# High and low matmuls of a split-precision recurrent block: alternating, or in runs of four, eight and sixteen

## The chip, the cores and the metric

The kernel runs on one core of a Trainium2 chip. The metric is the device time of one execution in microseconds (us). Profiles are of one execution. The engines are TensorE (PE, with its weight loads shown apart as PEld), VectorE (DVE), ScalarE (ACT), GpSimd (POOL) and SyncE (SP), which issues transfers.

## The reference, cut to what matters

The input x has 8 x 1024 rows of 256 float32 values. For each row:

```
xn = layernorm(x)
s  = rfs(xn) @ rfs(win)                       # random features, 256 x 256
h  = silu(xn @ w1.T * w1_s) * (xn @ w2.T * w2_s)   # gated layer, 256 -> 1024
h  = gelu(h @ h1.T * h1_s)                    # square layer, 1024 -> 1024
h  = gelu(h @ h2.T * h2_s)                    # square layer, 1024 -> 1024
y  = h @ w3.T * w3_s                          # last layer, 1024 -> 256
out = x + s * silu(y)
```

The weights w1, w2, h1, h2 and w3 hold only -1, 0 and 1. The result is wanted in float32 quality.

## The kernel before, in words

**Splitting.** Each activation is scaled and split into a high part (type float32r, made by ScalarE) and a low part (float16, made by VectorE as the value less its high part). Each product of the layers is then two matmuls into the same bank of PSUM: one with the high part and the weights as float32r, one with the low part and the weights read as bfloat16. The code calls them g = 0 and g = 1. The order of the two is what the change is about.

**Tiles.** A tile is 1024 rows, two halves of 512 (h0 and h1); eight tiles (t = 0 to 7) follow each other. In a tile TensorE goes through these stages, in one queue in this order:
- gated layer by seven products (`gate_seven`, line 850, all tiles but the first): the first half of the hidden columns, for both halves of rows, with Strassen's scheme. Products (p, n), p = 0 to 3 and n = 0 to 6, stand in eight rounds (`ROUNDS`): round i holds (0, i), (1, i), (2, i-1), (3, i-1), as far as n runs from 0 to 6. Each is one high and one low matmul of 512 columns. ScalarE copies the banks of n = 0, 2 and 4 out (lines 1077, 1079, 1081), VectorE adds others to them (1525, 1528, 1532). Product n = 5 waits for the copy of n = 4 of its p (`g3_kept`).
- gated layer by steps (`gate_step`, line 775): a step makes one block of 128 hidden columns for 512 rows: for each of w1 and w2 two high matmuls and then two low ones, into a pair of banks. ScalarE takes the silu (1066), VectorE multiplies (1514). Eight steps a tile, sixteen in the first.
- `dots` (860, the first tile only), `mix` (876) for s.
- two square layers (`product`, line 915), L = 0 and 1. Each is seven block products w = 0 to 6 (Strassen's scheme again, `FAST`): a 512 x 512 block of weights by 1024 rows folded to 512 columns. A product has four output blocks m (bank 4(w % 2) + m) by four contraction blocks k, by high and low: 32 matmuls of 512 columns. The weights of block k come in a piece of 256 KB in a ring of eight buffers, so a product's pieces are loaded while the one before it runs; a piece is given back (`piece_used`, `prod`) at its last use, and SyncE (GpSimd for some pieces of the first tile) then loads the piece of two products later (`feed`, line 453).
- last layer (`down`, line 972): four parts (b11, b22, b12, b21) of four blocks b of 128 rows by four k by high and low: matmuls of 256 columns whose stationary side is the activation. Between them, in all tiles but the last, seven float32 matmuls for the next tile's s (`seven`, lines 928 to 950).

**What a product's banks go through.** Products w = 0, 1 and 3 begin banks; w = 2 adds onto the banks of w = 0, w = 5 onto those of w = 3, and w = 4 and 6 onto those of w = 2. ScalarE copies the banks of w = 0, 2 and 4 to SBUF (`p1_kept`, `u2_kept`, `u3_kept`; lines 1171 to 1175); VectorE adds the bank of w = 1 (line 1590), that of w = 3 to the copy of w = 4 (line 1593, `c_sum["b22"]`), and that of w = 5 (line 1597); ScalarE applies gelu (lines 1163 and 1177). TensorE waits per m before it writes a bank: for w = 5 on `c_sum["b22"]` of m, which needs the copy of w = 4 of m, the product just before. For w = 0 of L = 1 it waits on the gelu of b21, which reads the banks of w = 6 of L = 0, again the product just before. For the others a whole product lies between.

**Order on ScalarE and VectorE.** Both go in program order, m by m: for m = 0 and 1 first the high (1119) or low (1557) split of half of the next product's operand, then the work on bank m of the current product, then the gelu of the block before. In L = 1 at m = 3 of w = 3 and 4 the split of b11 for the last layer stands ahead of the bank's work (`high_last`, line 1134; `low_last`, line 1563). On odd m of tiles 1 to 7, while there are any, ScalarE has a step of `look` (lines 1194 to 1200), which looks over the weights. VectorE has the layernorm of the next tile in L = 0 (`next_rows`; line 1419 normalises, at m = 2 and 3 of w = 4 two blocks each) in tiles 0 to 6.

The heart of `product`:

```
for m in range(Q):
    ... wait for bank m
    for k in range(Q):
        on.wait_ge(*fed[n])
        for g in range(2):
            ... matmul of (m, k), high for g = 0, low for g = 1
```

Of the kernel before, what the change touches and what calls it, by code (L numbers as in the profile page):

```python
# [5 lines left out]
P = 128  # L6
D = 256
# [93 lines left out]
def build(nc, x, win, proj, cols_in, w3s_in, wT, out):  # L101
# [4 lines left out]
    with ExitStack() as ctx:  # L106
# [647 lines left out]
        def _(e):  # L754
# [34 lines left out]
            def gate_step(t, n):  # L789
                h, m = step_of(t, n)  # L790
                pair = (PAIRS if t else PAIRS0)[n]
                on.wait_ge(rows_hi, n_rows_hi(h))
                if h == 0:
                    on.wait_ge(rows_hi0, 1)
                if t == 0:
                    for i in range(2):
                        on.wait_ge(d_w12[i][w12_part(m)], 16)
                gate_banks_free(t, n, 0)
                if h == 0 and m == 0:
                    gate_product(pair[0], w1, h, m, 0, True, False)  # L800
                    gate_product(pair[1], w2, h, m, 0, True, False)
                    on.wait_ge(rows_lo, n_rows_lo(h))
                    gate_product(pair[0], w1, h, m, 1, False, True).then_inc(gate_mm, 1)
                    gate_product(pair[1], w2, h, m, 1, False, True).then_inc(gate_mm, 1)
                else:
                    on.wait_ge(rows_lo, n_rows_lo(h))
                    gate_product(pair[0], w1, h, m, 0, True, False)
                    gate_product(pair[0], w1, h, m, 1, False, True).then_inc(gate_mm, 1)
                    gate_banks_free(t, n, 1)
                    gate_product(pair[1], w2, h, m, 0, True, False)  # L810
                    gate_product(pair[1], w2, h, m, 1, False, True).then_inc(gate_mm, 1)
# [10 lines left out]
            def gate_seven(t):  # L822
# [6 lines left out]
                for p, n in sum(ROUNDS, []):  # L829
# [3 lines left out]
                    if n < 2:  # L833
# [14 lines left out]
                    for g, (x_, T_) in enumerate(((xT_hi, T_hi), (xT_lo, T_lo))):  # L848
                        moving = (x_[0][:, 0, :], x_[0][:, 1, :], T_[:, 1, :], T_[:, 0, :], T_[:, 2, :], T_[:, 3, :], x_[1][:, 1, :])[n]
                        mm = e.matmul(ps[:, bank, :], short(weights) if g else weights, moving, start=n in (0, 1, 3) and g == 0, stop=n in (1, 5, 6) and g == 1,  # L850
                                      skip_group_check=True)
                    mm.then_inc(strassen_mm, 1)
# [27 lines left out]

            def product(t, L, w):
                slot = (t + L + w) % 2
                first, last = FAST[w][1] in ("b11", "b21", "t1"), w in (1, 5, 6)
                on.wait_ge(lo, n_split(t, L, w, 1))
                for m in range(Q):
                    if w == 0 and L == 0:
                        if t == 0:
                            on.wait_ge(*((turned_f, 4) if m < 2 else ((silu, gated)[m - 2], 2 * KH - 1)))
                        elif m % 2 == 0:
                            on.wait_ge(silu, n_step(t, 6 + m // 2))  # L890
                        else:
                            on.wait_ge(gated, n_gate(*step_of(t, 6 + m // 2)))
                    elif w == 0:
                        on.wait_ge(gelu["b21"], n_block(t, 0, m))
                    elif w == 1 and L == 0:
                        on.wait_ge(mixed, 4 * t + m + 1)
                    elif w == 1:
                        on.wait_ge(c_sum["b12"], n_block(t, 0, m))
                    elif w == 2:
                        on.wait_ge(p1_kept, n_block(t, L, m))  # L900
                    elif w == 3:
                        on.wait_ge(c_sum["b11"], n_block(t, L, m))
                    elif w == 4:
                        on.wait_ge(u2_kept, n_block(t, L, m))
                    elif w == 5:
                        on.wait_ge(c_sum["b22"], n_block(t, L, m))
                    else:
                        on.wait_ge(u3_kept, n_block(t, L, m))
                    for k in range(Q):
                        n = n_used(t, L, w, 0) // (Q - 1) * Q + k  # L910
                        on.wait_ge(*fed[n])
                        for g in range(2):
                            weights = ring[n % RING][:, m * P:(m + 1) * P]
                            weights, moving = (weights, slots_hi[slot][:, k, :]) if g == 0 else (short(weights), slots_lo[slot][:, k, :])
                            mm = e.matmul(ps[:, 4 * (w % 2) + m, :], weights, moving,  # L915
                                          start=first and k == 0 and g == 0, stop=last and k == Q - 1 and g == 1, skip_group_check=True)
# [36 lines left out]
            def down(t):  # L953
                begun = set()
                dot = 0
                for n, (name, j, kq) in enumerate(order_of(t)):
                    slot = last_slot(t, name)
                    on.wait_ge(last_lo, n_last(t, LAST[name], 1))
                    on.wait_ge(d_w3, 16)
                    last = j in begun  # L960
                    for b in range(NB):
                        bank, col = y_place(2 * t + j, b)
                        if not last and col == 0:
# [4 lines left out]
                        for k in range(Q):  # L968
                            for g in range(2):
                                tokens, moving = slice(b * P, (b + 1) * P), w3[:, Q * kq + k, :]  # L970
# [955 lines left out]
```

## Time and profile before

| | us |
|---|---|
| median of 3 runs | 1310.86 |
| lowest and highest | 1308.68, 1311.36 |
| the profiled execution | 1308.7 |
| its span, first to last instruction | 1306.9 |
| mean granted TensorE clock | 0.999 of full |
| TensorE busy in the span | 1296.6 (99%), 6010 matmuls |
| VectorE busy | 975.5 (75%) |
| ScalarE busy | 914.7 (70%) |
| GpSimd busy | 291.7 (22%) |

Busy times of matmuls overlap, since the end of one is recorded some 0.18 us after its last column went in, when the next already streams. The spacing of matmuls is therefore read from the chain that ended last: there each stretch of one engine and line stands with its start, its length and how many instructions it holds. In the tables, "idle before <-" names what ended the engine's idle time just before an instruction.

### The profile page before, as it was taken

How to read it: one execution, taken by the hardware profiler on the slowest of the kernel's cores; microseconds unless marked ns; L12 is line 12 of the kernel's file. 1: busy time of each engine (PE TensorE's matmuls, PEld its weight loads, DVE VectorE, ACT ScalarE, POOL GpSimd, SP SyncE). 2: the span in 40 equal slices, each digit the busy share in tenths (PEclk: the TensorE clock that was granted, in tenths of full speed). 3: DMA queues.
4: the chain of work that ended last, by engine and by line, in shares of the span. 5: the costliest groups of instructions: out<-in, count | busy, mean ns of one | idle time of the engine just before them, and what ended most of it. 6: DMA issues, size and time to landing. Idle time of an engine off the chain costs nothing.

```text
span 1306.9 us, 16520 instructions
## 1 busy us (share of the span) xinstructions
PE 1296.6 (99%) x6010; PEld 665.5 (51%) x6010; DVE 975.5 (75%) x1343; ACT 914.7 (70%) x1384; POOL 291.7 (22%) x323
## 2 busy tenths in 40 slices
PE   9999999999999999999999999999999999999998
PEld 5544455444554455544555445554455544554445
DVE  7778777777777787777876777767778677785675
ACT  5465666778667786677776777757777677686664
POOL 7875013110131101311023110322004120050000
PEclk9999999999999999999999999999999999999999
DMA  9689832575125741367414573146631566214441
GB/s 344 245 311 291 289 135 97 158 214 180 68 97 179 219 159 65 116 183 214 141 65 137 166 237 114 65 142 190 208 113 65 169 177 213 94 49 161 149 156 36
DMA packets 97350, 209.47 MB, mean 160 GB/s; under 512 B 13424, under 2 KB 16624, under 8 KB 96240
## 3 DMA queue, kind: packets, MB, share of 16 engines
q1 hardware_dynamic: 80032, 156.98, 36.2%
q0 software_dynamic: 17232, 51.39, 13.2%
q8 instruction: 49, 0.80, 0.2%
q14 instruction: 37, 0.30, 0.1%
HBM read 175.78 MB, written 38.83 MB: 164 GB/s over the span
## 4 chain that ended last, share of the span: by engine, by line
PE 98%; DMA 1%; DVE 1%; ACT 0%; issue 0%
PE ps L915 63%; PE ps L775 10%; PE ps L972 9%; PE ps L850 7%; PE ps L876 4%; DMA ring<-hs 1%; PE ps L860 1%; PE ps L950 0%; PE ps L939 0%; PE ps L928 0%; PE ps L943 0%; PE ps L936 0%; PE ps L947 0%; PE ps L931 0%; DMA xin<-in_x 0%; DVE split_lo L1563 0%
## 5 line engine op out<-in xcount | busy, mean ns | idle before, releaser
L915 PE MATMUL ps<-split_hi,ring 128*128 128x512 f32 x1792 | 833.2, 582 | 1.0 <-DMA ring<-hs 1.0
L915 PE MATMUL ps<-split_lo,ring 128*128 128x512 f16 x1792 | 700.1, 391 | 0.0
L1557 DVE SCALAR_TENSOR_TENSOR split_lo<-quad,split_hi 128x1024 f16<-128x1024 f32 x224 | 277.1, 1243 | 193.0 <-ACT split_hi L1119 193.0
L915 PEld LDWEIGHTS ps<-split_lo,ring 128*128 128x128 bf16 x1792 | 173.2, 97 | 460.1 <-issue 460.0
L915 PEld LDWEIGHTS ps<-split_hi,ring 128*128 128x128 f32 x1792 | 361.2, 202 | 1.6 <-DMA ring<-hs 1.3
L1119 ACT ACTIVATE split_hi<-quad 128x1024 fp32r<-128x1024 f32 x224 | 232.0, 1050 | 39.3 <-PE ps L915 39.3
L1163 ACT ACTIVATE quad<-quad,cols_s 128x512 f32<-128x512 f32 x192 | 135.4, 716 | 41.9 <-DVE quad L1590 22.6
L1582 DVE TENSOR_TENSOR quad<-quad 128x1024 f32<-128x1024 f32 x128 | 154.4, 1241 | 3.8 <-POOL res L616 3.7
L610 POOL TENSOR_TENSOR quad<-quad,s 128x256 f32<-128x256 f32 x56 | 61.8, 1133 | 426.8 <-ACT quad L1155 426.8
L775 PE MATMUL ps<-xT_hi,w 128*128 128x512 f32 x288 | 116.5, 486 | 0.8 <-ACT xT_hi L1222 0.8
L775 PE MATMUL ps<-xT_lo,w 128*128 128x512 f16 x288 | 87.5, 386 | 0.0
L972 PE MATMUL ps<-w,split_hi 128*128 128x256 f32 x272 | 79.7, 398 | 0.1
L596 POOL DMA_DIRECT2D z_h<-xin x56 | 55.6, 1000 | 105.0 <-DVE xin L1419 105.0
L1171 ACT ACTIVATE quad<-ps 128x512 f32<-128x512 f32 x64 | 38.2, 596 | 55.0 <-PE ps L915 54.8
L628 POOL DMA_DIRECT2D seen<-in_h x32 | 17.6, 550 | 246.0 <-ACT signs L1200 246.0
L972 PE MATMUL ps<-w,F_hi 128*128 128x256 f32 x240 | 70.0, 396 | 0.0
L972 PE MATMUL ps<-w,split_lo 128*128 128x256 bf16 x272 | 68.4, 288 | 0.0
L775 PEld LDWEIGHTS ps<-xT_hi,w 128*128 128x128 f32 x288 | 54.5, 190 | 20.3 <-ACT xT_hi L1222 1.0
L1066 ACT ACTIVATE rows<-ps,cols_s 128x512 f32<-128x512 f32 x72 | 49.7, 691 | 17.7 <-PE ps L775 11.5
L972 PE MATMUL ps<-w,F_lo 128*128 128x256 bf16 x240 | 60.4, 288 | 0.0
L972 PEld LDWEIGHTS ps<-w,split_hi 128*128 128x128 f32 x272 | 54.2, 199 | 6.9 <-issue 5.3
L1175 ACT ACTIVATE quad<-ps 128x512 f32<-128x512 f32 x64 | 38.2, 596 | 26.7 <-PE ps L915 25.1
(204 smaller groups left out, 1802.2 us busy)
## 6 DMA issues: line engine op xcount, KB each, us to landing
ring<-hs SPq DMA_DIRECT2D x428, 256.0 KB, 3.5
xin<-in_x SPq DMA_DIRECT2D x16, 512.0 KB, 4.3
s_h<-s SPq DMA_DIRECT2D x16, 512.0 KB, 4.1
seen<-in_h POOLq DMA_DIRECT2D x32, 256.0 KB, 3.9
res<-in_x SPq DMA_DIRECT2D x15, 512.0 KB, 5.4
out<-res SPq DMA_DIRECT2D x15, 512.0 KB, 2.9
z_h<-xin POOLq DMA_DIRECT2D x56, 128.0 KB, 4.2
xT_hi<-z_h POOLq DMA_DIRECT2D x14, 512.0 KB, 5.6
```

Source lines behind the costliest of these rows:

```text
L596: e.dma_start(z_h[j][:, :, :, c, :].rearrange("a i n j -> i n a j"), xin[j][32 * c:32 * c + 32, :, :].rearrange("i b (k a j) -> i (b k) a ...
L610: e.tensor_tensor(y_of(h)[:, b, :], y_of(h)[:, b, :], s[h % 2][:, b, :], ALU.mult).then_inc(pool_y, 1)
L775: mm = e.matmul(ps[:, bank, :], weights, moving, start=first and k == 0, stop=last and k == KD - 1, skip_group_check=h == 0 and m == 0)
L850: mm = e.matmul(ps[:, bank, :], short(weights) if g else weights, moving, start=n in (0, 1, 3) and g == 0, stop=n in (1, 5, 6) and g == 1, ...
L876: mm = e.matmul(ps[:, banks[b // 2], (b % 2) * D:(b % 2 + 1) * D], quad[at[t][0]["v"]][:, KD * j + r, b * P:(b + 1) * P], WS[:, r, :], sta ...
L915: mm = e.matmul(ps[:, 4 * (w % 2) + m, :], weights, moving, start=first and k == 0 and g == 0, stop=last and k == Q - 1 and g == 1, skip_g ...
L972: mm = e.matmul(ps[:, bank, col:col + D], part[:, k, tokens], moving, start=not last and col == 0 and k == 0 and g == 0, stop=last and k = ...
L1066: e.activation(stage[n % 2][:, :], ps[:, (PAIRS if t else PAIRS0)[n][0], :], ACT.Silu, scale=scale_col(0, m)).then_inc(silu, 1)
L1119: e.activation(both(slots_hi[i], g), both(quad[at[t][L][name]], g), ACT.Identity, scale=POWER[L]).then_inc(hi, 1)
L1163: e.activation(q[:, m, :], q[:, m, :], ACT.Gelu, scale=col).then_inc(gelu[name], 1)
L1557: e.scalar_tensor_tensor(out=both(slots_lo[i], g), in0=both(quad[at[t][L][FAST[w][1]]], g), scalar=POWER[L], in1=both(slots_hi[i], g).bitc ...
L1582: e.tensor_tensor(dst, a, b, ALU.subtract).then_inc(block_sum, 1)
```

## The change

The loops over g (high, low) go outward.
- Square layers: all 16 high matmuls of a product, then all 16 low ones. The waits for the banks stand in the high run, in the order of m; the wait for the low split stands before the low run, and the product begins after the high split alone. A bank is handed on (`prod`) after its last low matmul, and pieces are given back in the low run of m = 3.
- Last layer: for each two blocks b, eight high matmuls, then eight low ones.
- Gated layer by steps: the four high matmuls of w1 and w2, then the four low ones; the second bank is waited for after two matmuls rather than four. The very first step was so already, but for the wait's place.
- Gated layer by seven: a round's high matmuls (four, two in the first and the last round), then its low ones, with the waits in the high run.

What is computed, and how many instructions there are, stays.

```diff
@@ gate_step
-                if h == 0 and m == 0:
...
-                else:
-                    on.wait_ge(rows_lo, n_rows_lo(h))
-                    gate_product(pair[0], w1, h, m, 0, True, False)
-                    gate_product(pair[0], w1, h, m, 1, False, True).then_inc(gate_mm, 1)
-                    gate_banks_free(t, n, 1)
-                    gate_product(pair[1], w2, h, m, 0, True, False)
-                    gate_product(pair[1], w2, h, m, 1, False, True).then_inc(gate_mm, 1)
+                gate_product(pair[0], w1, h, m, 0, True, False)
+                gate_banks_free(t, n, 1)
+                gate_product(pair[1], w2, h, m, 0, True, False)
+                on.wait_ge(rows_lo, n_rows_lo(h))
+                gate_product(pair[0], w1, h, m, 1, False, True).then_inc(gate_mm, 1)
+                gate_product(pair[1], w2, h, m, 1, False, True).then_inc(gate_mm, 1)
@@ gate_seven
-                for p, n in sum(ROUNDS, []):
+                for p, n, g in [(p, n, g) for turn in ROUNDS for g in range(2) for p, n in turn]:
...
-                    if n < 2:
+                    if g:
+                        pass
+                    elif n < 2:
                         first_free(t, bank)
...
-                    for g, (x_, T_) in enumerate(((xT_hi, T_hi), (xT_lo, T_lo))):
...
-                    mm.then_inc(strassen_mm, 1)
+                    x_, T_ = (xT_lo, T_lo) if g else (xT_hi, T_hi)
...
+                    if g:
+                        mm.then_inc(strassen_mm, 1)
@@ product (the waits on banks, unchanged, are now bank_free)
-                on.wait_ge(lo, n_split(t, L, w, 1))
-                for m in range(Q):
...
+                on.wait_ge(hi, n_split(t, L, w, 1))
+                for m, g in [(m, g) for g in range(2) for m in range(Q)]:
+                    if g == 0:
+                        bank_free(t, L, w, m)
                     else:
-                        on.wait_ge(u3_kept, n_block(t, L, m))
+                        on.wait_ge(lo, n_split(t, L, w, 1))
                     for k in range(Q):
                         n = n_used(t, L, w, 0) // (Q - 1) * Q + k
                         on.wait_ge(*fed[n])
-                        for g in range(2):
...
-                        if k == Q - 1:
+                        if g and k == Q - 1:
                             mm.then_inc(prod, 1)
-                        elif m == Q - 1:
+                        elif g and m == Q - 1:
                             mm.then_inc(piece_used, 1)
@@ down
-                    on.wait_ge(last_lo, n_last(t, LAST[name], 1))
+                    on.wait_ge(last_hi, n_last(t, LAST[name], 1))
                     on.wait_ge(d_w3, 16)
                     last = j in begun
-                    for b in range(NB):
+                    for b, g in [(b, g) for two in (0, 2) for g in range(2) for b in (two, two + 1)]:
                         bank, col = y_place(2 * t + j, b)
-                        if not last and col == 0:
+                        if g:
+                            on.wait_ge(last_lo, n_last(t, LAST[name], 1))
+                        elif not last and col == 0:
...
-                            for g in range(2):
...
-                        mm.then_inc(down_mm, 1)
-                        if b % 2 and t < END and dot < 7:
-                            seven(t, dot)
-                            dot += 1
+                        if g:
+                            mm.then_inc(down_mm, 1)
+                            if b % 2 and t < END and dot < 7:
+                                seven(t, dot)
+                                dot += 1
```

## Rows read from the trace of the kernel before

**Rows 1.** The page, parts 1 and 4: busy us, share and count; the chain by engine.
```profile
PE 1296.6 (99%) x6010; PEld 665.5 (51%) x6010; DVE 975.5 (75%) x1343; ACT 914.7 (70%) x1384; POOL 291.7 (22%) x323
...
PE 98%; DMA 1%; DVE 1%; ACT 0%; issue 0%
```

**Rows 2.** TensorE's waits (us in total, times, longest), and the ring's transfers.
```profile
PE ps L915 <- DMA ring<-hs: 1.0, 1, 1.0
...
DMA to landing us min/median/max: 2.6/3.5/9.8
```

**Rows 3.** The chain in order of time, tiles 3 and 4: start us, us, what.
```profile
538.84 104.03 PE ps L915 x448
642.87 1.97 PE ps L972 x16
...
664.67 13.01 PE ps L850 x56
677.68 14.60 PE ps L775 x64
```

**Rows 4.** Timeline of TensorE: the first step's low run, and one low matmul.
```profile
10.39 1.04 PE L775 MATMUL ps<-xT_lo,w 128*128 128x512 f16 x4
...
600.21 0.39 PE L915 MATMUL ps<-split_lo,ring 128*128 128x512 f16 x1
```

**Rows 5.** Timeline of ScalarE, tile 3, L = 1, around the end of w = 4.
```profile
626.18 0.60 ACT L1175 ACTIVATE quad<-ps 128x512 f32<-128x512 f32 x1
626.68 0.71 ACT L1163 ACTIVATE quad<-quad,cols_s 128x512 f32<-128x512 f32 x1
627.29 1.05 ACT L1134 ACTIVATE F_hi<-quad 128x1024 fp32r<-128x1024 f32 x1
628.24 0.59 ACT L1175 ACTIVATE quad<-ps 128x512 f32<-128x512 f32 x1
628.71 0.72 ACT L1163 ACTIVATE quad<-quad,cols_s 128x512 f32<-128x512 f32 x1
629.33 0.62 ACT L1200 ACTIVATE signs<-seen 128x512 bf16<-128x512 f32 x1
629.85 0.20 ACT L1200 ACTIVATION_READ_ACCUMULATOR signs<-seen 128x1 f32 x1
```

**Rows 6.** Timeline of VectorE in the same stretch.
```profile
623.75 0.68 DVE L1593 TENSOR_TENSOR quad<-ps,quad 128x512 f32<-128x512 f32 x1
624.35 1.22 DVE L1557 SCALAR_TENSOR_TENSOR split_lo<-quad,split_hi 128x1024 f16<-128x1024 f32 x1
...
628.37 1.23 DVE L1563 SCALAR_TENSOR_TENSOR F_lo<-quad,F_hi 128x1024 f16<-128x1024 f32 x1 [0.86 <-ACT F_hi L1134]
629.51 0.69 DVE L1593 TENSOR_TENSOR quad<-ps,quad 128x512 f32<-128x512 f32 x1
```

**Rows 7.** The chain in order of time, tile 0, the transfer of a piece.
```profile
86.28 9.76 DMA ring<-hs
```

**Rows 8.** Timeline of TensorE: the matmul that this transfer released.
```profile
96.09 0.50 PE L915 MATMUL ps<-split_hi,ring 128*128 128x512 f32 x1 [1.01 <-DMA ring<-hs]
```

**Rows 9.** Timeline of VectorE, tile 3, L = 0: two normalisations and what follows.
```profile
582.89 0.73 DVE L1419 TENSOR_SCALAR xin<-xin,mv,sm 128x256 f32<-128x256 f32 x2
583.54 0.69 DVE L1597 TENSOR_TENSOR quad<-ps,quad 128x512 f32<-128x512 f32 x1
```

**Rows 10.** Timeline of ScalarE in the gated layer by seven products, tile 4.
```profile
671.72 1.09 ACT L1081 ACTIVATE quad<-ps 128x512 f32<-128x512 f32 x2
```

**Rows 11.** The chain in order of time, the last tile's last layer.
```profile
1285.98 2.37 DVE split_lo L1563 x2
1288.35 0.04 issue
```

**Rows 12.** Weight loads of the last layer by form; transposes in the chain.
```profile
L972 PEld LDWEIGHTS ps<-w,F_hi 128*128 128x128 f32 x240 | 47.9, 200 | 5.1 <-issue 5.1
...
15.09 0.87 PE ps L768 x8
```

More of the change, by code:

```diff
@@ L879, in mix, with bank_free @@
                         mm.then_inc(mix_mm, 1)
+            def bank_free(t, L, w, m):
+                if w == 0 and L == 0:
+                    if t == 0:
+                        on.wait_ge(*((turned_f, 4) if m < 2 else ((silu, gated)[m - 2], 2 * KH - 1)))
+                    elif m % 2 == 0:
+                        on.wait_ge(silu, n_step(t, 6 + m // 2))
+                    else:
+                        on.wait_ge(gated, n_gate(*step_of(t, 6 + m // 2)))
+                elif w == 0:
+                    on.wait_ge(gelu["b21"], n_block(t, 0, m))
+                elif w == 1 and L == 0:
+                    on.wait_ge(mixed, 4 * t + m + 1)
+                elif w == 1:
+                    on.wait_ge(c_sum["b12"], n_block(t, 0, m))
+                elif w == 2:
+                    on.wait_ge(p1_kept, n_block(t, L, m))
+                elif w == 3:
+                    on.wait_ge(c_sum["b11"], n_block(t, L, m))
+                elif w == 4:
+                    on.wait_ge(u2_kept, n_block(t, L, m))
+                elif w == 5:
+                    on.wait_ge(c_sum["b22"], n_block(t, L, m))
+                else:
+                    on.wait_ge(u3_kept, n_block(t, L, m))
             def product(t, L, w):
@@ L911, in product @@
                         on.wait_ge(*fed[n])
-                        for g in range(2):
[L913 to L916, printed above, removed]
-                        if k == Q - 1:
+                        weights = ring[n % RING][:, m * P:(m + 1) * P]
+                        weights, moving = (weights, slots_hi[slot][:, k, :]) if g == 0 else (short(weights), slots_lo[slot][:, k, :])
+                        mm = e.matmul(ps[:, 4 * (w % 2) + m, :], weights, moving,
+                                      start=first and k == 0 and g == 0, stop=last and k == Q - 1 and g == 1, skip_group_check=True)
+                        if g and k == Q - 1:
                             mm.then_inc(prod, 1)
-                        elif m == Q - 1:
+                        elif g and m == Q - 1:
                             mm.then_inc(piece_used, 1)
@@ L968, in down @@
                         for k in range(Q):
[L969 to L978 removed]
+                            tokens, moving = slice(b * P, (b + 1) * P), w3[:, Q * kq + k, :]
+                            part, moving = (slots_hi[slot], moving) if g == 0 else (slots_lo[slot], short(moving))
+                            mm = e.matmul(ps[:, bank, col:col + D], part[:, k, tokens], moving,
+                                          start=not last and col == 0 and k == 0 and g == 0, stop=last and k == Q - 1 and g == 1,
+                                          skip_group_check=True)
+                        if g:
[3 more added lines that the diff above has]
+                                dot += 1
                     begun.add(j)
```

36 lines of the change are left out of this document (3 added, 33 removed).

## The prediction

> **What bounds the kernel now.** The page's first part comes first: TensorE is busy for 99% of the span, VectorE for 75%, ScalarE for 70% [rows 1]. The chain that ended last says the same: 98% of it is TensorE [rows 1]. In the table of waits TensorE waits once for a piece of weights (1.0 us) and hardly elsewhere [rows 2]. So the time is the number of matmuls times their spacing, and the change touches both sides: the spacing (which kind follows which), and the distance between the matmul that ends a bank and the one that needs it again.
>
> The spacing stands in the chain in order of time [rows 3]. Square layers: 448 matmuls, 224 pairs of high and low in turn, take 104.03 us, 0.4644 us a pair. Second half of the gated layer: 64 matmuls in runs of two (two high, two low), 14.60 us, 0.4563 a pair or 0.9125 for four. Both orders hold one high-to-low and one low-to-high step per run; the run of two adds one high-after-high and one low-after-low, together 0.9125 - 0.4644 = 0.448. The kernel's first step has a run of four lows [rows 4]: 1.04 us, less 0.39 for one alone, over three steps: 0.217. So high after high is 0.231, and a change of kind costs about 0.008 each way.
>
> **What the longer runs give.** All on TensorE, which sets the end.
> - Square layers: a product of 32 matmuls goes from 7.430 to 0.464 + 15 x 0.448 = 7.186; 0.244 x 112 products = 27.4 us.
> - Gated layer by steps: 1.825 to 0.464 + 3 x 0.448 = 1.809; 0.016 x 71 steps = 1.1 us (one step had this order already).
> - Gated layer by seven products: 28 pairs took 13.01 us [rows 3]. The rounds hold 2, 4 (six times) and 2 pairs: 2 x 0.9125 + 6 x 1.809 = 12.68; 0.33 x 7 tiles = 2.3 us.
> - Last layer: 256 columns, 1.97 us for 8 pairs, 0.2466 a pair [rows 3]; 64 runs of eight. No row has two highs in a row at 256 columns. If a step saves the same 16 ns: 7 x 64 x 0.0163 = 7.3 us; if it halves with the columns, 3.7. I take 5.5, between them. The bound the other way is a rival below.
> Sum: 36.3 us off. The instructions are the same in number, on every engine and queue; TensorE's waits are moved, none is new in kind.
>
> **What it puts in their place.** A bank now ends late. In a product, bank m ended after 8(m+1) of 32 matmuls; now in the low run, after 20, 24, 28 and 32. It is still asked for early, at the product's high run, now at matmul 4m instead of 8m. Where the next product takes the same values on, the distance falls from 24 matmuls (5.6 us) to 12 (2.7 us). That is product w=5 of a layer, which waits for c_sum b22 of the same m: ScalarE copies bank m of w=4 (L1175), VectorE adds (L1593). I walk both queues in program order by the starts in the rows (one start to the next): copy 0.49, gelu 0.61, high split 0.95, look 0.52, VectorE's sum 0.60, low split 1.14 [rows 5, 6]. With E = 0 the end of w=4, banks end at -2.59, -1.73, -0.86, 0. From a release to the end of the matmul that waited is 0.54 us [rows 7, 8] (landing 86.28 + 9.76 = 96.04, record from 96.09, 0.50 long), against 0.23 in the stream, so bank m must be free by 0.93m - 0.30.
> - Layer 2 (L=1). ScalarE: copy 0 at -2.56, high split of w=5, copy 1 at -1.11, gelu, look, copy 2 at 0.52, gelu, then the split of b11 for the last layer (L1134, [rows 5]) 1.62 to 2.67, copy 3 at 2.57. VectorE: low split until 0.17, sum 1 done 0.86 (wanted 0.63), sum 2 done 1.84, then L1563 from 2.70, which waits for that split, and sum 3 done 4.53, wanted 2.48. TensorE stands 0.2 at m=1 and 1.8 at m=3: 2.05 us. Six tiles 12.3, the last (no looks) 1.9, the first (small sums of the projection before sum 2) 2.3: 16.5 us.
> - Layer 1 (L=0). No such split, but two normalisations (L1419, 0.73 for both, 0.64 without the overlap with what follows) before each of sums 2 and 3 [rows 9]: done 0.86, 2.11, 3.36 against 0.63, 1.56, 2.48; 0.88 us in tiles 1 to 6, 0.3 in the last: 5.6. In tile 0 it hides behind the piece (below).
> - Layer 1's w=6 to layer 2's w=0 use one bank as well (gelu b21, then reuse); that walk ends at 0.28, 1.49, 2.07 against 0.63, 1.56, 2.48: nothing, by under 0.1 us. The split of w=1 and of w=3 lands within 0.1 us of its need; nothing too. What covers these is ScalarE being free; if it slips 0.3 us, each costs that.
> - Gated layer by seven: n=5 follows n=4 of its p by one round and needs the copy L1081. The distance falls from 6 matmuls (1.4 us) to 3 (0.7), the copy alone takes 0.60, two together 1.09, so they follow each other by 0.48 [rows 10], and both p of a round wait: 0.30 + 0.26 in round 5, 0.25 + 0.26 in round 6, 1.07 us; x 7 = 7.5. The other waits there are 11 matmuls (2.5 us) and hold.
> - Tile 0: the piece that lands at 96.04 after 9.8 us is the fourth of w=5 [rows 7]. It was wanted after six matmuls, now after three, and TensorE comes 1.5 us sooner. It stands until 96.04 again, has 29 matmuls to go, not 26, and the gains up to there (1.8 us) are lost; the fourth piece of layer 2's w=0 repeats it. 2.6 us in all (between 1, if the transfer starts and lands sooner with the product that frees its buffer, and 4).
> - Later tiles: ring releases bunch at the product's end, up to 0.7 us later, wanted up to 0.7 sooner; median landing is 3.5 us [rows 2] of a product's 7.2. Nothing. Waiting for the high split alone at a product's start, and for the low one 3.7 us later, removes a need that cost nothing.
> - The last tile waited for low splits at 1288.35 in the last layer [rows 11]; with gelus of b21 bunched it waits 0.3 us more.
> Sum: 16.5 + 5.6 + 7.5 + 2.6 + 0.3 = 32.5 us on.
>
> **The number.** 36.3 off and 32.5 on: 3.8 us less. The profiled execution took 1308.7 (span 1306.9 and 1.8 around it); 1304.9 in its place. The median shown, 1310.86, lies 2.2 above it, so 1307.
>
> **Rivals.**
> 1. The waits hardly appear (12%): the queues catch up, or a wait is overlapped as the walk does not see. Against it: the walk uses starts of one execution and strict program order. 36.3 less some 10 gives 1285, all of it 1275.
> 2. Slower: in the last layer a high load does not fit behind 256 columns (10%). The records of high loads last 200 ns [rows 12]; if the next matmul must wait for load and hand-over, high after high is 0.23, as at 512 columns, a pair 0.23 + 0.109 = 0.34 instead of 0.2466, and 448 such steps cost 41 us: 1354. It decides from a pair of about 0.243, where the forecast gain is gone. Against it: eight transposes of 128 float32 columns, each with a load of its own, take 0.87 us, 0.109 each [rows 12], and in the alternating order a load of each kind fits in 0.2466 with a matmul that alone takes half of that. The Trainium skill (TensorE: Matmul & The Clock Gate, LDWEIGHTS) gives columns over 1.2 GHz, an estimate of 107 ns for 128 columns; by it this rival falls, and the records' 200 ns include more than the load.
> 3. Slower: the bunched banks push ScalarE and VectorE behind by more than I walked (18%), at the three places with under 0.1 us to spare. 0.3 us at each, some 40 times, is 12 us: 1319.
> 4. Order does not set the spacing (3%): both orders would have one pair time and only the waits stay, less the 1.8 of gains that tile 0 then has not to lose: 1342. The two pair times in rows 3 speak against it. The Trainium skill (same page, Back-to-back issue gap) has columns over 2.4 GHz plus 2.5 ns whatever the order, 216 ns at 512; the low run's 0.217 agrees, the high run's 0.231 and the alternating 0.232 do not.
> That the order is not what the code says is excluded: one queue, one order.
>
> **How the numbers follow.** The forecast case, waits and gains within a quarter of the walk, has 57% and reaches from 16 us faster to 4 slower, 1295 to 1315. 0.2% is 2.6 us, about what can be told from no change. Three fifths of that case lie beyond it on the fast side, a quarter inside. That gives 0.34 faster, 0.14 same and 0.09 slower; rival 1 adds 0.12 to faster, rivals 2 and 4 0.13 to slower, and rival 3 0.14 to slower and 0.04 to same: 0.46, 0.18, 0.36. The range takes in rival 3 and the near part of rival 1: 1291 to 1320.
>
> **What would show it.** In the chain, a product of w=0 to 4 near 7.19 us; among the waits a new row of L1593 releasing the square layers' matmuls, some 20 us, longest near 1.8, in pairs of places 52 us apart; a second of L1081 releasing the seven products, some 7 us; runs of 16 in the last layer near 1.88 us. A last-layer run at 2.6 would be rival 2; idle time under 10 us on TensorE rival 1; square products at 7.43 without waits rival 4; many short waits for the high split L1119 rival 3.

## The result, and the profile after

| us | before | after |
|---|---|---|
| median of 8 runs each, in turn on one chip | 1309.36 | 1314.78 |
| lowest and highest | 1308.47, 1311.36 | 1312.04, 1317.24 |
| the profiled execution | 1308.7 | 1312.04 |
| its span | 1306.9 | 1310.2 |

The ratio is 1.0038, 95% interval 1.0026 to 1.005: slower by 5.4 us, and beyond the 0.2% of the prediction. Forecast were 1307 and "faster" as the likeliest. The result lies inside the range, on its other side.

TensorE's share fell from 99% to 97%, and the chain that ended last, 98% TensorE before [rows 1], now passes through ScalarE, VectorE and the DMA queues. From the page of after, parts 1 and 4:

```profile
PE 1277.2 (97%) x6010; PEld 813.4 (62%) x6010; DVE 973.5 (74%) x1343; ACT 906.0 (69%) x1384; POOL 294.6 (22%) x323
...
PE 81%; ACT 6%; DVE 6%; DMA 4%; issue 1%; SPq 1%; ACTq 0%; DVEq 0%
```

TensorE's waits of after (us in total, times, longest). Where [rows 2] has a single row for the ring, these matter:

```profile
PE ps L917 <- DVE quad L1597: 13.4, 11, 1.5
PE ps L917 <- DMA ring<-hs: 5.6, 6, 1.8
PE ps L917 <- ACT split_hi L1123: 1.8, 6, 0.8
...
PE ps L975 <- ACT quad L1181: 1.0, 1, 1.0
```

The table undercounts: a matmul held up by less than its own recorded length (0.4 to 0.5 us) shows no idle time. So a wait is read here from how long a product takes, from the end of the last matmul before it to its own last. The windows below are cut at those ends: tile 3, L = 1, products w = 1 to 6 of after. Behind each stretch stands its length (the product's time), then TensorE's busy time; then weight loads, VectorE, ScalarE, GpSimd, the granted clock, the DMA share and GB/s.

```profile
600.76:607.90 7.14, 7.14 (x33) 4.47 (x33) 6.30 (x8) 4.93 (x9) 1.52 (x3) 1.00 0.99 288
607.90:617.00 9.10, 7.70 (x33) 4.43 (x33) 3.79 (x5) 5.47 (x10) 0.00 (x0) 1.00 0.55 174
617.00:624.14 7.14, 7.14 (x32) 4.15 (x31) 5.08 (x6) 4.99 (x9) 0.54 (x1) 1.00 0.71 226
624.14:631.73 7.59, 7.39 (x33) 4.75 (x34) 7.59 (x8) 5.73 (x11) 0.00 (x0) 1.00 0.49 168
631.73:640.96 9.23, 7.73 (x34) 4.26 (x33) 7.16 (x10) 8.20 (x15) 0.00 (x0) 1.00 0.36 115
640.96:648.07 7.11, 7.11 (x35) 4.50 (x34) 3.76 (x6) 5.36 (x9) 0.00 (x0) 1.00 0.45 148
```

An undisturbed product takes 7.14 us, where it took 7.43 (104.03 / 14, [rows 3]). Three here take longer: w = 2 (9.10), w = 4 (7.59) and w = 5 (9.23); in L = 0 only w = 5 does, 8.06. Only w = 5 was forecast. Added up over the 112 products of the profiled execution (each less 7.14):

| place | waits, us | forecast |
|---|---|---|
| w = 5 of L = 1, eight tiles | 16.8 | 16.5 |
| w = 5 of L = 0, tiles 1 to 7 | 5.9 | 5.6 |
| w = 5 of L = 0, tile 0 (not a piece, see below) | 2.2 | 2.6 more than before's 1.3, with the next row |
| w = 0 of L = 1, tile 0 (not a piece) | 1.1 | in the row above |
| w = 2 of L = 1, tiles 1 to 6 | 7.6 | nothing |
| w = 4 of L = 1, tiles 1 to 6 | 2.6 | nothing |
| single pieces (w = 4 of L = 1 in tile 0, w = 3 in tile 6) | 0.4 | nothing |

112 products save 0.29 each, 32.5 us. The table comes to 36.6 (small differences of other products are 0.1), and before itself had 1.3 of waits in tile 0. So the square layers came out 2.7 us longer.

In tile 0 the waits for a piece that were forecast did not come: the fourth piece of w = 5 of L = 0 landed at 93.3, 6.6 us after its issue, for 96.04 before. TensorE waited at the same places for VectorE and ScalarE. TensorE's waits of after, in the window 90 to 112:

```profile
PE ps L917 <- DVE quad L1597: 1.4, 2, 0.7
PE ps L917 <- ACT split_hi L1123: 0.8, 1, 0.8
```

Ahead of each of the sums of banks 2 and 3, VectorE has four statistics of the next tile's rows there (L1429 and L1430, 1.3 us for four). Ahead of w = 0 of L = 1, four normalisations (L1423, 1.4 us) stand before a sum (L1601), and the gelu and the high split that TensorE waits for follow that sum.

The rest of the span's 3.3: the stages between the square layers are 0.2 shorter after each of six tiles and 0.3 longer after tile 0, those ahead of the first square layer take 0.8 more, the end 0.6 more.

The rest of the forecast, in the chain of after in order of time, tiles 3 and 4, beside [rows 3]:

```profile
648.07 1.87 PE ps L975 x16
...
669.08 8.14 PE ps L845 x36
677.22 0.04 issue
677.26 2.79 PE ps L845 x10
680.06 2.79 PE ps L845 x10
682.84 14.46 PE ps L775 x64
```

The last layer's run of 16 fell from 1.97 to 1.87, and the steps from 14.60 to 14.46. The seven products rose from 13.01 to 13.77 (from 669.08 to 682.84): the chain breaks up where n = 5 waits for the copy of n = 4, L1085 (L1081 before). Such waits lengthen 28 steps of the seven tiles, by 7.7 us together.

The profiled execution is the fastest of after's eight, 2.7 us below the median, while before's is 0.7 below its own. What the other seven spent more is in no trace; their mean granted clock is on record, 0.997 to 0.999 for the profiled 0.999. An estimate: 0.001 less over 1310 us is worth 1.3 us, so it can be a good part of the difference (the last section has such stretches).

### The profile page after: what moved, and what is told of

Its sections match the earlier page's. It is cut to its first block, busy times and chain, and to the rows that moved or that the text cites. A ratio compares the mean times of both kernels' runs of the same rounds, so it can differ in the third digit from the quotient of the medians.

```text
span 1310.2 us, 16520 instructions
## 1 busy us (share of the span) xinstructions
PE 1277.2 (97%) x6010; PEld 813.4 (62%) x6010; DVE 973.5 (74%) x1343; ACT 906.0 (69%) x1384; POOL 294.6 (22%) x323
## 4 chain that ended last, share of the span: by engine, by line
PE 81%; ACT 6%; DVE 6%; DMA 4%; issue 1%; SPq 1%; ACTq 0%; DVEq 0%
PE ps L917 48%; PE ps L775 9%; PE ps L975 9%; PE ps L845 7%; PE ps L872 4%; DMA ring<-hs 3%; ACT split_hi L1123 2%; DVE quad L1597 1%; ACT quad L1179 1%; DVE split_lo L1561 1%; ACT quad L1167 1%; DVE F_lo L1567 1%; DMA quad<-in_win 1%; DVE xin L1423 1%; SPq L453 1%
## 5 line engine op out<-in xcount | busy, mean ns | idle before, releaser
L917 PE MATMUL ps<-split_hi,ring 128*128 128x512 f32 x1792 | 462.1, 406 | 21.6 <-DVE quad L1597 13.4
L1561 DVE SCALAR_TENSOR_TENSOR split_lo<-quad,split_hi 128x1024 f16<-128x1024 f32 x224 | 279.4, 1253 | 183.0 <-ACT split_hi L1123 182.7
L917 PEld LDWEIGHTS ps<-split_hi,ring 128*128 128x128 f32 x1792 | 331.4, 188 | 123.3 <-DVE quad L1597 32.3
L917 PE MATMUL ps<-split_lo,ring 128*128 128x512 f16 x1792 | 406.4, 380 | 0.0
L1123 ACT ACTIVATE split_hi<-quad 128x1024 fp32r<-128x1024 f32 x224 | 233.7, 1054 | 25.2 <-PE ps L917 23.3
L775 PE MATMUL ps<-xT_hi,w 128*128 128x512 f32 x288 | 91.6, 439 | 0.8 <-ACT xT_hi L1226 0.8
L596 POOL DMA_DIRECT2D z_h<-xin x56 | 55.7, 1001 | 123.4 <-DVE xin L1423 123.4
L775 PE MATMUL ps<-xT_lo,w 128*128 128x512 f16 x288 | 74.7, 382 | 0.0
L1070 ACT ACTIVATE rows<-ps,cols_s 128x512 f32<-128x512 f32 x72 | 49.7, 691 | 21.4 <-PE ps L775 12.6
L1567 DVE SCALAR_TENSOR_TENSOR split_lo<-quad,split_hi 128x1024 f16<-128x1024 f32 x34 | 40.8, 1221 | 29.3 <-ACT split_hi L1138 29.3
L1597 DVE TENSOR_TENSOR quad<-ps,quad 128x512 f32<-128x512 f32 x64 | 43.7, 685 | 23.2 <-ACT quad L1179 23.2
L1181 ACT ACTIVATE quad<-ps,cols_s 128x512 f32<-128x512 f32 x64 | 41.7, 684 | 25.9 <-PE ps L917 25.9
L616 POOL TENSOR_TENSOR res<-res,quad 128x256 f32<-128x256 f32 x56 | 58.3, 1072 | 1.1
L872 PE MATMUL ps<-WS,quad 128*128 128x256 f32 x256 | 56.7, 379 | 0.2 <-ACT quad L1281 0.2
```

The costliest lines, as they stand in the source:

```text
L616: e.tensor_tensor(res[:, b, :], res[:, b, :], y_of(h)[:, b, :], ALU.add).then_inc(pool_out, 1)
L775: mm = e.matmul(ps[:, bank, :], weights, moving, start=first and k == 0, stop=last and k == KD - 1, skip_group_check=h == 0 and m == 0)
L872: mm = e.matmul(ps[:, banks[b // 2], (b % 2) * D:(b % 2 + 1) * D], quad[at[t][0]["v"]][:, KD * j + r, b * P:(b + 1) * P], WS[:, r, :], sta ...
L917: mm = e.matmul(ps[:, 4 * (w % 2) + m, :], weights, moving, start=first and k == 0 and g == 0, stop=last and k == Q - 1 and g == 1, skip_g ...
L1123: e.activation(both(slots_hi[i], g), both(quad[at[t][L][name]], g), ACT.Identity, scale=POWER[L]).then_inc(hi, 1)
L1561: e.scalar_tensor_tensor(out=both(slots_lo[i], g), in0=both(quad[at[t][L][FAST[w][1]]], g), scalar=POWER[L], in1=both(slots_hi[i], g).bitc ...
```

## The experiments

Four accounts of the lost gain stood against each other: the forecast waits of w = 5 and of the seven products eat it; waits at the places that were costed at nothing, w = 2 and w = 4 of L = 1, eat it; the longer run brings less spacing than reckoned, so that shorter runs would be no better; the last layer's high runs cost something. Every median stands beside runs of before on the same chip. Those lie at 1309.36 to 1309.66 throughout, so that medians of different kernels can be set side by side to some tenths.

**Undo one part: the seven products alternate again.** Waits stay where they are.

```diff
-                for p, n, g in [(p, n, g) for turn in ROUNDS for g in range(2) for p, n in turn]:
+                for p, n in sum(ROUNDS, []):
...
+                    for g, (x_, T_) in enumerate(((xT_hi, T_hi), (xT_lo, T_lo))):
```

> The changed kernel with the gated layer by seven products in its old order (high and low of a product in turn). Theory (bunched banks): the seven products took 13.76 us a tile changed against 13.01 before, so seven tiles give 0.75 x 7 = 5 us back: the changed kernel's 1314.8 less 5, about 1310, and no wait of L845 left. Rival (the time comes from the weight pieces alone): only the spacing gain of this stage is lost, 0.33 x 7 = 2.3 us, so 1317.

Measured 1307.18 (12 runs, 1303.03 to 1315.6; before 1309.43, ratio 0.999, 0.9974 to 1.0006), 7.6 less than after. In its chain the seven products are one piece again:

```profile
505.04 12.97 PE ps L843 x56
```

That is 0.8 a tile, 5.5 in seven. The part is a loss of the size walked. The other 2 us may be chance: this kernel's runs spread by 12 us, and their mean granted clock from 0.999 to 0.995 in the longest.

**Move one cover: b11's splits behind the bank's work.** The kernel after, but the high and low split of b11 for the last layer (w = 3 and 4 of L = 1, m = 3) go behind `product_out`, so the copy and the sum that TensorE waits for come first.

```diff
+                            product_out(t, L, w, m)
                             if L == 1 and m == 3 and w in (3, 4):
                                 high_last(t, "b11", w - 3)
-                            product_out(t, L, w, m)
@@ VectorE the same, with low_last
```

> The changed kernel with the split of b11 for the last layer (high on ScalarE, low on VectorE) behind the bank's work at m=3 of w=3 and w=4 instead of ahead of it. Theory (bunched banks): product w=5 of L=1 falls from 9.2 to about 7.6 us, so 1.6 x 8 = 13 us off: 1302. Rival (the queues are simply too full): the time of the split is paid at the next wait, and the total stays at 1315, with a new wait of similar size in w=5, w=6 or the last layer.

Measured 1302.22 (before 1309.43, ratio 0.9949, 0.9936 to 0.9962), 12.6 less than after. Its waits, and w = 5 of L = 1 in tile 3 (9.23 in after):

```profile
PE ps L917 <- DMA ring<-hs: 6.0, 6, 1.8
PE ps L917 <- DVE quad L1597: 2.4, 3, 1.0
...
628.60:636.24 7.64, 7.63 (x33) 4.26 (x33) 5.79 (x8) 7.30 (x13) 0.00 (x0) 1.00 0.44 139
```

1.6 us in seven tiles and 0.8 in tile 0 are 11.9 of the 12.6: the largest wait is what it was forecast to be, the split of b11 ahead of one copy and one sum. The run moves both halves of the split, so it does not tell ScalarE's part from VectorE's. With it alone mended, the sixteens beat the kernel before. The waits in w = 2 are untouched (8.4 us in this execution, 7.6 in after's).

**Change one size: runs of four, and of eight.** In both the seven products alternate and the steps and the last layer are as changed. Fours are the high and then the low matmuls of one m, eights those of two.

```diff
-                for m, g in [(m, g) for g in range(2) for m in range(Q)]:
+                for m, g in [(m, g) for m in range(Q) for g in range(2)]:
@@ eights
+                for m, g in [(m, g) for two in (0, 2) for g in range(2) for m in (two, two + 1)]:
```

> Square layers in runs of four (four highs of a bank, then its four lows), the gated layer by seven in its old order, the steps and the last layer as changed. A bank ends and is wanted where it was before the change. Theory: a product takes 4 x (0.464 + 3 x 0.445) = 7.20 us and has no bank wait: 112 x 0.23 = 26 us, with 6 of the last layer and 1 of the steps 33 off the kernel before: 1276, or up to 1283 if the late release of the weight pieces (still in the low run of m=3) keeps its waits of some 7 us in w=2 of L=1. Rival (runs only pay when long): runs of four gain less than half of what sixteen do, 1295 or more.

> As the run of fours, but the square layers in runs of eight: the highs of banks 0 and 1, their lows, then banks 2 and 3. The distance from a bank's end to its next need is 20 matmuls (24 before, 12 in the change). Theory: 7.16 us a product and still no bank wait by the walk of the queues (sum 3 of w=4 done 3.2 us into the next product, wanted at 4.2): 1272, or up to 1280 with waits for pieces. Rival (any loss of distance costs): w=5 of L=1 waits a microsecond, and the total is above that of the fours.

Fours 1283.29 (ratio 0.9802, 0.9789 to 0.9816), eights 1277.85 (0.9767, 0.9755 to 0.978), before 1309.43. The square layers of tile 2 in the chain, one unbroken piece each (104.03 before); of the fours:

```profile
373.19 101.17 PE ps L914 x448
...
495.37 13.00 PE ps L843 x56
```

and of the eights:

```profile
372.62 100.52 PE ps L914 x448
```

A product takes 7.226 and 7.180, where 7.20 and 7.16 were expected. From tile 1 on every product of both takes this, but one of 7.22. So the longer run does bring its spacing: eights have 0.25 us of the 0.29 that sixteens gain a product, and none of their waits. The last step, from 7.18 to 7.14, is worth 4.5 us. It brings some 33 us of waits: the 36.6 of the table, where the eights have 3.5, all in tile 0 and nearly all for pieces.

**Only the last layer.** The kernel before, with the last layer in runs of eight.

> The kernel before with the last layer alone in runs of eight. Theory: 8 pairs of 256 columns take 1.875 us instead of 1.973, 64 times: 6.3 us off, 1303, with no new wait but 0.3 us in the last tile. Rival (the last layer's gain in the changed kernel came from what ran beside it): less than 3 us off.

Measured 1303.93 (4 runs; before 1309.51, ratio 0.9953, 0.9938 to 0.9968): 5.6 us, where the prediction had 5.5. The last layer's runs of 16 stand in the chain at 1.87 or 1.88, as

```profile
487.61 1.87 PE ps L973 x16
490.34 1.88 PE ps L973 x16
```

The last layer is a gain, and rival 2 falls.

**Why w = 2 waits: hold the rows' transfers back.** VectorE's last normalisations of the next tile's rows stand in its queue between its work on the banks of L = 0's w = 6, which now end together at the product's end. The last of them starts at 272.67 for 269.16 in tile 1. It is what GpSimd's next transfer waits for, which sends the rows to DRAM (L596); L603 then reads them back transposed. GpSimd's timeline, tile 1, of before, then of after (in brackets what it waited for):

```profile
270.39 3.96 POOL L596 DMA_DIRECT2D z_h<-xin  x4 [5.65 <-DVE xin L1419]
274.34 0.56 POOL L603 DMA_DIRECT2D xT_hi<-z_h  x1
...
279.66 0.54 POOL L603 DMA_DIRECT2D xT_hi<-z_h  x1
```

```profile
273.90 3.96 POOL L596 DMA_DIRECT2D z_h<-xin  x4 [7.34 <-DVE xin L1423]
277.85 0.57 POOL L603 DMA_DIRECT2D xT_hi<-z_h  x1
...
282.04 0.54 POOL L603 DMA_DIRECT2D xT_hi<-z_h  x1 [1.81 <-DMA z_h<-xin]
```

The rows leave 3.5 us later (3.0 against the end of L = 0's w = 6), and the four pieces of L = 1's w = 2, issued from 277.2 to 278.8, fly beside them and what follows them on GpSimd's queue. The ring's issues in 270 to 290, to landing, of before and of after:

```profile
DMA to landing us min/median/max: 3.6/4.1/5.5
```

```profile
DMA to landing us min/median/max: 3.0/5.4/8.6
```

The chain of after holds the worst, the piece k = 3 that w = 2 of tile 1 stood for:

```profile
278.77 8.56 DMA ring<-hs
287.33 0.04 issue
```

Two runs test this from both sides. In the first, the kernel after, GpSimd waits for the last bank of L = 1's w = 1 before a block of weights for `look` and the transposed read of the second half's rows go out:

```diff
                     rows_in(h0 + 2)
+                    on.wait_ge(prod, n_prod(t, 1, 1, Q - 1))
                     load_looked(begin + 5, begin + 6)
                     rows_in(h1 + 2)
```

> The changed kernel, but GpSimd holds one looked-over piece of weights and the second half's rows (xT_hi) back until product w=1 of L=1 has ended; until then only the first half's rows and the ring load. Theory (collision): the changed kernel waits 0.8 to 2.0 us in w=2 of L=1 of tiles 1 to 4 and 6 for its weight pieces, because the rows' transfers start 7.2 us after the end of w=6 instead of 4.2 and meet the ring's; with two of them held the waits shrink to under half of their 7.6 us: 1308 to 1311 for 1314.8. Rival (the ring's requests, bunched at a product's end, are slow by themselves): the pieces land as late, the waits stay, 1315.

Measured 1310.22 (11 runs; before 1309.51, ratio 1.0001, 0.9992 to 1.001), 4.6 below after. The waits for the ring:

```profile
PE ps L918 <- DMA ring<-hs: 2.2, 4, 1.0
```

w = 2 waits 3.7 us in tiles 1 to 6, for 7.6. But w = 3 now waits 1.5, for 0.2, so a part only moved: the two together are 5.2 for 7.8. In tile 0, where the edit does nothing, w = 5 took 11.14 for 9.50 in this execution, with a granted clock of 0.85 in it, so the profile shows less gain than the median. The run holds back two transfers at once and does not say which of them mattered.

In the second, the fours, which have no such wait, get after's lateness alone: GpSimd sends the second half's rows only once bank 1 of L = 1's w = 0 is done.

```diff
                     load_looked(begin + 4, begin + 5)
+                    on.wait_ge(prod, n_prod(t, 1, 0, 1))
                     rows_out(h1 + 2)
```

> The square layers in runs of four (no waits of their own from tile 1 on), with the second half's rows sent out by GpSimd 3.6 us after the end of w=6 instead of 0.4 us, as VectorE's lateness does in the changed kernel. Theory (collision): waits for pieces appear in w=2 of L=1, 0.5 to 2 us a tile in tiles 1 to 6: 3 to 10 us above the fours' 1283.3. Rival (it takes the long runs): no waits of L914 for the ring, 1283.

Measured 1294.85 (4 runs; before 1309.51, ratio 0.9892, 0.9877 to 0.9907), 11.6 above the fours. Its waits:

```profile
PE ps L915 <- DMA ring<-hs: 8.5, 9, 1.7
```

The products w = 2 of L = 1 take 9.42, 11.73, 9.23, 8.56, 7.85 and 9.22 us in tiles 1 to 6, the others 7.23: 12.6 us, more than the 3 to 10 expected. So late rows, with what follows them on GpSimd's queue, are enough to make this wait, without any longer run, and at a place where nothing on TensorE or in its queue was changed. The 11.73 holds more than waits (see the last section).

**Why w = 4 waits: move one high split.** In after, VectorE's late low split of w = 3 delays the next rows' sums and transposes, and ScalarE's high split of these rows (L1063) stands ahead of the high split of w = 4. The chain of after, tile 3:

```profile
617.77 1.22 DVE quad L1586
618.99 1.23 DVE xin L1503 x2
620.22 0.02 issue
620.24 1.06 ACT xT_hi L1063
...
623.24 1.05 ACT split_hi L1123
624.29 0.04 issue
624.34 4.82 PE ps L917 x20
```

TensorE stands at 624.14 with w = 3 done, and goes on from 624.34. The run: after, with this L1063 moved from m = 3 of w = 2 to m = 2 of w = 3.

```diff
-                            if 0 < t < END and (L, w, m) in ((1, 2, 3), (1, 6, 2)):
-                                rows_high(h0 + 2 + (w == 6))
+                            if 0 < t < END and (L, w, m) == (1, 6, 2):
+                                rows_high(h0 + 3)
+                            if 0 < t < END and (L, w, m) == (1, 3, 2):
+                                rows_high(h0 + 2)
```

> The changed kernel with ScalarE's high split of the next tile's rows (first half) moved from ahead of bank 3's copy in w=2 of L=1 to w=3, behind both high splits of w=4. Theory (a chain): w=4 of L=1 takes 7.6 us in tiles 1 to 6 because that split waits for VectorE's transposes, VectorE being late after the low split of w=3, and the high split of w=4 queues behind it; moved, w=4 takes 7.14 and 0.46 x 6 = 2.8 us go: 1312. Rival (VectorE is late by itself, for the subtraction that w=4 needs): w=4 stays at 7.6, 1315.

Measured 1310.91 (12 runs, 1307.09 to 1314.76; before 1309.66, ratio 1.0004, 0.9984 to 1.0024), 3.9 below after. In its profile w = 4 takes 7.14 in every tile; tile 3:

```profile
624.44:631.58 7.14, 7.14 (x34) 4.48 (x33) 5.66 (x6) 3.62 (x6) 0.00 (x0) 1.00 0.44 147
```

for 7.59. That is the table's 2.6 us. Its w = 2 took 8.67, 11.32, 8.24, 7.62, 7.55 and 8.64, 9.2 us of waits for the 7.6 of after.

**All four mended together.** Sixteens with the seven products in turn, b11's splits behind, the rows held and L1063 moved.

> Runs of sixteen with the four mendings together: the seven products in their old order, the split of b11 behind the bank's work, the second half's rows and a looked-over piece held back, the rows' high split moved. Theory: the causes add: 1314.8 less 12.6, 7.6, 4.6 and 2.8 is 1287, within 3 us; what is left above the eights' 1277.9 is the 0.9 and 0.5 us a tile of w=5 and some waits for pieces. Rival (they share one cause): less than 20 us off, 1295 or more.

Measured 1293.76 (4 runs, 1289.18 to 1295.4; before 1309.66, ratio 0.9884, 0.987 to 0.9898): above the 1287 and its margin, and 21.0 below after for the 27.6 expected. The profiled execution is the lowest of the four (1289.18); there w = 5 keeps 0.9 in L = 0 and 0.5 in L = 1, the ring's pieces still cost up to 1.8 in w = 2 or 3 of L = 1 (4.8 in all), and tile 0 has 4.9 of waits, nearly all for VectorE and ScalarE:

```profile
PE ps L915 <- DVE quad L1597: 2.4, 3, 1.0
PE ps L915 <- DMA ring<-hs: 2.0, 4, 0.9
```

By the profiles the four do add up. There they are worth 11.9 (w = 5), 5.4 (the seven products), 2.6 (w = 2 and 3) and 2.6 (w = 4), 22.5 together, and this profiled execution is 22.9 below after's. The medians of single mendings had shown more than their places did (7.6 for 5.4, 4.6 for 2.6, 3.9 for 2.6). The four still leave the sixteens 16 us above the eights.

**The eights with the seven products in runs of two.** A run of two there keeps a round's first two products apart from its last two.

> The runs of eight, and in the gated layer by seven runs of two (a round's first two products high, high, low, low, then its other two). Theory: 28 pairs at 0.456 instead of 0.464 save 0.23 us a tile, and n=5 keeps five matmuls of distance from n=4, which the copies of 0.6 and 1.1 us just fit in: 1.6 less at most 0.7 us for 1277.9, so about 1277, not to be told from it. Rival (distance of three was not the cause of the waits in L845): waits like those of the changed kernel, 0.75 us a tile or more.

Measured 1277.01 (before 1309.51, ratio 0.9755, 0.9742 to 0.9769), not to be told from the eights' 0.9767. The seven products take what they took:

```profile
494.60 13.00 PE ps L845 x56
```

The 0.23 us a tile that the runs of two were to give are lost again: in each tile the second high matmul of n = 5 comes 0.38 us after the one before it in round 5, released by the copy L1085, and 0.30 in round 6, for 0.23.

The two eights are the fastest kernels of this study, 2.3 and 2.4% below before.

## Why the prediction failed

**The mechanism held, and all priced terms but two (tile 0 and the size of the spacing gain).** The walk of the two queues behind w = 4 of L = 1 gave 2.05 us a tile, measured 2.09 (9.23 less 7.14); for L = 0 0.88, measured 0.92. It can be laid on the timeline. With w = 4 ending at 631.73, it had the sum of bank 2 done at 633.57, L1567 (before: L1563) from 634.43 and the sum of bank 3 done at 636.26. VectorE of after:

```profile
632.86 0.69 DVE L1597 TENSOR_TENSOR quad<-ps,quad 128x512 f32<-128x512 f32 x1 [0.26 <-ACT quad L1179]
634.42 1.23 DVE L1567 SCALAR_TENSOR_TENSOR F_lo<-quad,F_hi 128x1024 f16<-128x1024 f32 x1 [0.87 <-ACT F_hi L1138]
635.56 0.68 DVE L1597 TENSOR_TENSOR quad<-ps,quad 128x512 f32<-128x512 f32 x1
```

The ends are 633.55, 635.65 and 636.24. The seven products were forecast at 12.68 + 1.07 = 13.75 and took 13.77; the last layer's run at 1.887 (1.973 less 5.5/64) and took 1.875.

**Tile 0's term came near by luck.** It added 2.0 (3.3 less 1.3) for the 2.6 forecast, but no piece was in it. "It stands until 96.04 again" failed, since the piece landed at 93.3. So did "In tile 0 it hides behind the piece": the next rows' statistics on VectorE held up the sums of w = 5, and its normalisations the first high split of L = 1.

**The spacing gain was sized too small**, 7.186 a product for 7.14. The step that mis-sized it is "high after high is 0.231" plus 0.217 for low after low. In the high runs of the square layers, matmuls follow each other by 0.228 us (median) and in the low runs by 0.216, 0.444 together where two runs of [rows 3] gave 0.448. The rows were read rightly. But they show only the first step of a high run, and the step shrinks along the run: the second to the fourth matmul come after 0.229, 0.236 and 0.233, the eleventh to the sixteenth after 0.227. So the steps (1.808 measured, 1.809 forecast) and the seven products (12.68 without their waits) came out as walked, and only the runs of sixteen gained more. Over 112 products it is 5 us. All spacing gains together are 32.5 + 6.2 (last layer) + 1.3 (steps) + 2.3 (seven products) = 42.3 us, for 36.3. The split of the price was wrong too: "a change of kind costs about 0.008 each way", while nearly all of it is at the low matmul (last section). The Trainium skill (TensorE: Matmul & The Clock Gate, Back-to-back issue gap) gives 216 ns at 512 columns for the isolated gap, by the columns alone; the low run agrees, the high run is 10 to 20 ns above it.

**Two sentences that ended in "nothing" failed, and with them the sign.** The waits came to some 46 us for 32.5 (3.3 longer, and 42.3 of gains): 35.3 in the square layers, 7.6 in the seven products (5.3 longer and 2.3 of gain), some 2.5 at the start and the end.
- "Later tiles: ring releases bunch at the product's end ... median landing is 3.5 us of a product's 7.2. Nothing." The distance was judged by a median landing, which holds while nothing else moves. Here 7.6 us. The runs show that the bunched releases alone are not the cause: the fours give their pieces back over the last four matmuls as well, wait for none from tile 1 on, and take 12.6 us once their rows leave late. What failed is a step that was not walked at all: who is fed by VectorE besides TensorE. The normalisations between the late banks came 3 us later, and with them a train of transfers.
- "The split of w=1 and of w=3 lands within 0.1 us of its need; nothing too. What covers these is ScalarE being free". The low split itself did not hold TensorE. Behind it on VectorE stood the rows' sums and transposes, behind these L1063, and behind L1063 the high split of the *next* product. Here 0.3 to 0.5 us in each of six tiles. The walk stopped at the instruction TensorE waits for, instead of following what is queued behind it.

Both are rival 3 in kind (bunched banks push the engines behind by more than walked, the time above before), with 18%: its places were near but not these, and most of its cost went through transfers, which it did not name. Its price, 12 us, was about what came (10.6), which is luck too. The mark set for it, many short waits for L1123, shows as 1.8 us in six (one of them, 0.8, in tile 0).

**The rivals.** Rival 1 (waits hardly appear) fell in the profile of after. Rival 2 fell by the last layer alone, 5.6 us faster. At 256 columns high after high takes 0.119, where it priced 0.23. Rival 4 fell by the unbroken 101.17 and 100.52. A forecast case 20 us wide, built on a difference of two sums of 36 and 32, should have put the sign nearer to even than 0.46 to 0.36.

**What stays open.** After's median stands 2.7 us above its profiled execution. That w = 2 varies from execution to execution is likely, since the profiles of three kernels with the same orders around it have 8.98, 9.44 and 11.32 us for it in tile 2 (after, b11's splits moved, L1063 moved), but the other runs of each have no trace. Which of the transfers on GpSimd's queue lengthens the pieces' landing is open, and so is why the step of a high run shrinks along it. A ring of more buffers was not tried.

## What to carry to other kernels

Grouping matmuls of one kind pays about in proportion to the changes of kind that go, so most of it comes with runs of four to eight: here 0.20, 0.25 and 0.29 us a product for runs of four, eight and sixteen, with 24, 28 and 30 of 32 changes gone. What it costs depends on how long a bank stays open past the point where the next user asks for it: lengthen runs only as far as that distance stays above the copy and sum that free the bank. When a bank comes late, follow every queue behind the engine that waits for it to its last consumer, the transfers that it feeds included, and judge a transfer's landing by what will fly beside it then.

## What the hardware showed that was not expected

**The two kinds have different spacing.** In the square layers of after, medians between ends: at 512 columns high after high 0.228 us (0.233 in the runs of four of the steps), low after low 0.216; high to low 0.233, low to high 0.229. In the last layer, at 256 columns, 0.119, 0.113, 0.131 and 0.115. In both, nearly the whole cost of a change of kind sits on the step from high to low. Of the 0.29 us a product, about 0.26 come from 15 of 16 low matmuls taking 0.216 for 0.233, and 0.03 from the high ones.

**Waits can be followed by a stretch at half clock.** In tile 2 of the fours with late rows, TensorE was busy for 1.15 of 3.50 us in the first window below, with two waits of 1.9 and 1.05 in it; the granted clock of the next 3.5 us was 0.53, near the level of 1.2 GHz, and nine matmuls took them, 0.39 each. Then it was back:

```profile
440.00:443.50 3.50, 1.15 (x5) 0.40 (x3) 1.75 (x3) 2.28 (x4) 0.00 (x0) 1.00 1.14 259
443.50:447.00 3.50, 3.50 (x9) 1.96 (x9) 0.52 (x1) 1.19 (x3) 0.00 (x0) 0.53 0.73 247
447.00:455.00 8.00, 8.00 (x37) 4.57 (x36) 4.94 (x6) 6.07 (x11) 0.54 (x1) 0.99 0.33 107
```

The 11.32 of the kernel with L1063 moved has the same mark, after 2.23 us busy of 4.00:

```profile
446.00:450.00 4.00, 2.23 (x8) 1.35 (x8) 2.25 (x4) 2.72 (x5) 0.00 (x0) 0.96 0.87 275
450.00:455.00 5.00, 5.00 (x17) 3.26 (x16) 0.98 (x1) 0.44 (x1) 0.00 (x0) 0.69 0.27 102
```

The waits of these two products were 3.0 and 2.6 us, and the matmuls at 0.43 behind them, for 0.23, added some 1.5 each: 4.5 and 4.2 above their kind. The profiled run of the last layer alone has a third case, in w = 5 of L = 0 of tile 0: a wait of 2.5 for a piece, then 3.50 us at a granted clock of 0.53, and 11.71 for the product (8.70 before). Not every such wait does it: in w = 2 of after, with waits of 2.0 and 1.8 us in tiles 1 and 2, the granted clock was 1.00.
